# Mixture-of-experts block: experts in units of two or three tiles with the up weights stationary, and one loop body on TensorE

## The reference

```python
x = x + attention(layernorm(x), ctx, ctx)        # 16 heads, projections with bias
xf = layernorm(x).reshape(-1, 256)               # 2048 tokens
probs = softmax(xf @ router_w + router_b)        # 8 experts
top_w, top_idx = top_k(probs, 2)
comb = sum(top_w[..., None] * one_hot(top_idx, 8), axis=1)
out = 0
for e in range(8):
    h = gelu(xf @ expert_up[e].T)                # 256 -> 1024
    out = out + comb[:, e:e+1] * (h @ expert_down[e].T)   # 1024 -> 256
x = x + out.reshape(4, 512, 256)
```

## Time and profile before

| what | us |
|---|---|
| median of three runs (417.35 to 422.19) | 420.72 |
| profiled execution | 422.39 |
| its span | 420.6 |
| PE busy in the span | 385.4 |

### The profile page before, as it was taken

One profiled execution on the slowest core, in us unless ns is written; L12 is line 12 of the kernel. 1 busy time (PEld: TensorE's weight loads), 2 busy tenths in 40 slices (PEclk: granted clock), 3 DMA queues, 4 the chain that ended last, 5 costly groups with the idle time before them and its releaser, 6 DMA issues.

```text
span 420.6 us, 9003 instructions
## 1 busy us (share of the span) xinstructions
PE 385.4 (92%) x2227; PEld 313.0 (74%) x2228; DVE 240.0 (57%) x691; ACT 195.9 (47%) x357; POOL 164.7 (39%) x253
## 2 busy tenths in 40 slices
PE   8989988988988889898999999999999999999960
PEld 6765675665675469896888888888888888888850
DVE  5674776899799767762337636473723643332320
ACT  3545444343434247334447647474734744443420
POOL 2332121211302031146454655655464464546441
PEclk9989999998999999989999999999999999999996
DMA  8912010410221111642326656564632222222121
GB/s 271 348 48 100 0 52 0 153 50 2 71 81 51 51 54 52 199 100 44 52 40 200 169 144 142 137 175 110 196 81 38 38 40 49 37 39 38 38 38 12
DMA packets 26388, 37.22 MB, mean 88 GB/s; under 512 B 4704, under 2 KB 17440, under 8 KB 26368
## 3 DMA queue, kind: packets, MB, share of 16 engines
q1 hardware_dynamic: 19312, 26.98, 18.9%
q0 software_dynamic: 7056, 9.99, 14.8%
HBM read 27.18 MB, written 9.79 MB: 88 GB/s over the span
## 4 chain that ended last, share of the span: by engine, by line
PE 74%; DVE 11%; SPq 4%; ACT 4%; issue 3%; DMA 2%; POOL 1%; POOLq 0%; DVEq 0%; ACTq 0%
PE bankC L1577 14%; PE bankC L1220 10%; PE bankC L1222 10%; PE bankC L1221 10%; PE bankC L1578 7%; PE bankB L1555 6%; PE bankA L1314 2%; PE bankA L1547 2%; PE bankB L1315 1%; PE bankC L1302 1%; DVE nmax L791 1%; DVE put L956 1%; DMA raw<-down 1%; DVE at_l L822 1%; DVE av L817 1%
## 5 line engine op out<-in xcount | busy, mean ns | idle before, releaser
L1577 PE MATMUL bankC<-dn_w,qk_h 128*128 x256 | 94.4, 407 | 1.2 <-DVE qk_l L1155 1.2
L1578 PE MATMUL bankC<-dn_w,qk_l 128*128 x256 | 71.9, 281 | 0.0
L460 POOL DMA_INDIRECT out<-x2T,idx_s x32 | 51.5, 1610 | 18.6 <-issue 18.6
L1577 PEld LDWEIGHTS bankC<-dn_w,qk_h 128*128 128x128 f32 x256 | 48.2, 188 | 11.6 <-issue 1.4
L1220 PE MATMUL bankC<-up_w,xnT_h 128*128 (+1 forms) x128 | 53.1, 415 | 1.0 <-DVE xnT_l L1149 1.0
L1222 PE MATMUL bankC<-up_w,xnT_l 128*128 (+1 forms) x128 | 50.7, 396 | 0.0
L1162 DVE SCALAR_TENSOR_TENSOR x2T<-bankC,gate,x2T 128x256 f32<-128x256 f32 x32 | 15.4, 482 | 61.7 <-ACT x2T L682 52.9
L1221 PE MATMUL bankC<-up_w,xnT_h 128*128 (+1 forms) x128 | 50.6, 395 | 0.0
L1578 PEld LDWEIGHTS bankC<-dn_w,qk_l 128*128 128x128 f32 x256 | 48.2, 188 | 0.0
L677 ACT ACTIVATE raw<-bankC 128x512 f32<-128x512 f32 x64 | 38.4, 599 | 20.3 <-PE bankC L1222 20.3
L450 POOL DMA_INDIRECT xr<-rows,idx_g x35 | 38.9, 1112 | 19.4 <-issue 19.4
(11 more groups left out here) (259 smaller groups left out, 824.1 us busy)
## 6 DMA issues: line engine op xcount, KB each, us to landing
xall<-up SPq DMA_DIRECT2D x24, 256.0 KB
xall<-down SPq DMA_DIRECT2D x24, 256.0 KB
rows<-xr SPq DMA_DIRECT2D x4, 528.0 KB, 3.3
raw<-up SPq DMA_DIRECT2D x4, 512.0 KB, 4.7
raw<-down SPq DMA_DIRECT2D x4, 512.0 KB, 5.3
out<-xall SPq DMA_DIRECT2D x4, 512.0 KB, 2.8
xall<-x SPq DMA_DIRECT2D x1, 1536.0 KB, 9.1
cst<-const SPq DMA_DIRECT2D x1, 640.0 KB, 8.1
```

The source lines that it names most:

```text
L460: g.indirect_dma_start(out, bass.IndirectOffsetOnAxis(idx_s[:, n:n + 1], 0), y[n], None, bounds_check=T + P - 1, compute_op=ALU.add).then_ ...
L1577: mm(bankC[:, 2, :], hT_h[:, o], wd, start=(m == 0), stop=False)
L1578: last = mm(bankC[:, 2, 0:D], hT_l[:, o], wd[:, 0:D], start=False, stop=(m == KF - 1))
```

## The change

Tiles of an expert are grouped: two tiles to a unit, and three in the first unit of an expert with an odd number. Each unit gathers three tiles (a two-tile unit doesn't use the third) and transposes all three. In the up product the weights are stationary and x moves, in 256 or 384 columns, so h comes out with hidden features on its partitions and needs no transposes: per unit 8 x 2 x 3 = 48 matmuls, in four quarters over four banks. ACT takes the gelu twice, rounded to fp32r (high part) and in f32, and DVE subtracts (low part). In the down product the 512-column matmul is split in two of 256, so a tile has 24 matmuls; it accumulates all in one place and ACT's part in the result goes. PE's loop holds one unit: four copies of the up part, one per combination of weight buffer and number of tiles, of which a compare picks one (so their addresses need no registers), two copies of the transposes of x, and a down part per tile with the buffer in a register. The PSUM banks, some buffers, the table and the order of gathers and adds change with it: the third gather of a unit is issued between adds, `add_early(0, 1)` moves behind the first gather, and the first transposes of x move between the two last early down parts.

```diff
-NTAB = NT + 3
+NU = NT // 2
+NTAB = NU + 4
+TRI = 3 * P
...
+        hh, hl = sb("hh", [P, KF * TRI], F32R), sb("hl", [P, KF * TRI], F32R)
...
+        bankC = ps("bankC", [P, 4, 512])
+        bankD = ps("bankD", [P, 2, 512])
+        bankB0, bankB1, bankM = bankC[:, 3, :], bankD[:, 0, :], bankD[:, 1, :]
...
+            def fetch(ring, t):
+                n = 3 * ring + t
+                g.indirect_dma_start(xr[:, n, :], None, rows, bass.IndirectOffsetOnAxis(idx_g[:, n:n + 1], 0),
                                      bounds_check=T + P - 1).then_inc(d_gather[ring], 16)
...
+            def add(u, ring, nth):
+                gather_index(u + 3, 1 - ring, nth)
...
+                pool.wait_ge(d_add, 16 * base + 64)
+                g.tensor_copy(idx_s[:, 3 * ring:3 * ring + 3], slot[:, bass.ds(col, 3)]).then_inc(g_si, 1)
+                pool.wait_ge(g_si, u + 1)
+                pool.wait_ge(v_y, 2 * u + 3)
+                settle(17)
+                give(ring, 0)
+                fetch(1 - ring, 0)
+                pool.wait_ge(v_y, 2 * u + 4)
+                pool.wait_ge(d_add, 16 * base + 80)
+                settle(18)
+                give(ring, 1)
+                fetch(1 - ring, 1)
+                with pool.If(three > 0):
+                    pool.wait_ge(d_add, 16 * base + 96)
+                    settle(19)
+                    give(ring, 2)
+                fetch(1 - ring, 2)
...
             gather(0, 0, 0, col=2)
+            add_early(0, 1)
             pool.wait_ge(v_tab, 1)
+            nu = pool.value_load(nu_i, min_val=NE, max_val=NU)
+            gather(1, 1, 0)
+            add_early(1, 0)
             gather(2, 0, 1)
             add_early(1, 1)
...
+            def gelu(u, n):
+                for q in range(4):
+                    act.wait_ge(p_up, 4 * u + q + 1)
+                    bank = bankC[:, 2 * (q % 2):2 * (q % 2) + 2, 0:n * P]
+                    a.activation(hT_h[:, 2 * q:2 * q + 2, 0:n * P], bank, ACT.Gelu)
+                    a.activation(hbuf[q][:, :, 0:n * P], bank, ACT.Gelu).then_inc(a_gelu, 1)
...
+            def h_low(u, n):
+                for q in range(4):
+                    dve.wait_ge(a_gelu, 4 * u + q + 3)
+                    v.tensor_tensor(hT_l[:, 2 * q:2 * q + 2, 0:n * P], hbuf[q][:, :, 0:n * P],
+                                    hT_h[:, 2 * q:2 * q + 2, 0:n * P].bitcast(F32), ALU.subtract).then_inc(v_fhT, 1)
...
+            def unit(u, ring, nth):
...
+                with dve.If(three > 0):
+                    h_low(u, 3)
+                with dve.Else():
+                    h_low(u, 2)
+                x_low_f(u + 1, 1 - ring, nth)
+                with dve.If(sp_e > 1):
+                    weights_low(sp_e, other, 0)
+                dve.wait_ge(p_dn0, u + 1)
+                dve.wait_ge(d_add, 16 * done + 64)
+                result(ring, 0).then_inc(v_y, 1)
+                with dve.If(sp_e > 1):
+                    weights_low(sp_e, other, 1)
+                dve.wait_ge(p_dn, u + 1)
+                settle(16)
+                with dve.If(three > 0):
+                    result(ring, 2)
+                result(ring, 1).then_inc(v_y, 1)
...
             up_early(1, 3)
             down_early(1, 0)
+            x_turn_f(0, 0)
             down_early(1, 1)
...
+            def up_product(u, par, n):
+                for q in range(4):
+                    pe.wait_ge(a_gelu, 4 * u + q + 1)
+                    for m in (2 * q, 2 * q + 1):
+                        w = slice(m * P, (m + 1) * P)
+                        for k in range(KD):
+                            last = three(bankC[:, 2 * (q % 2) + m % 2, 0:n * P], up_w[:, 0, par, k, w],
+                                         up_w[:, 1, par, k, w], xT_h[:, k, 0:n * P], xT_l[:, k, 0:n * P],
+                                         k == 0, k == KD - 1)
                     last.then_inc(p_up, 1)
+            def down_tile(u, par, t, first):
+                out_ = bankD[:, (t + 1) // 2, t // 2 * D:(t // 2 + 1) * D]
                 for m in range(KF):
+                    if first and m % 2 == 0:
+                        pe.wait_ge(v_fhT, 4 * u + m // 2 + 1)
+                    o = slice(t * P, (t + 1) * P)
+                    w_h, w_l = (dn_w[:, bass.ds(par, 1), m, part, :].rearrange("p a n -> p (a n)") for part in range(2))
+                    mm(out_, hT_h[:, m, o], w_h, start=(m == 0), stop=False)
+                    mm(out_, hT_h[:, m, o], w_l, start=False, stop=False)
+                    last = mm(out_, hT_l[:, m, o], w_h, start=False, stop=(m == KF - 1))
+                return last
...
             pe.wait_ge(v_tab, 1)
+            nu = pe.value_load(nu_i, min_val=NE, max_val=NU)
+            with pe.Fori(0, NU) as u:
+                with pe.If(nu > u):
+                    word = pe.value_load(w_i[:, bass.ds(u, 1)], min_val=0, max_val=4 * NE - 1)
+                    e, three_, par = word // 4, word // 2 % 2, word % 2
+                    pe.wait_ge(v_wlo, 4 * e + 2)
+                    pe.wait_ge(v_fxT, u + 1)
+                    for n in (2, 3):
+                        for p in range(2):
+                            with pe.If(word % 4 == 2 * (n - 2) + p):
+                                up_product(u, p, n)
+                    for ring in range(2):
+                        with pe.If(u % 2 != ring):
+                            x_turn_f(ring, (u + 1) // 2)
+                    pe.wait_ge(v_wlo, 4 * e + 4)
+                    pe.wait_ge(v_y, 2 * u + 2)
+                    with pe.If(three_ > 0):
+                        down_tile(u, par, 2, True)
+                    down_tile(u, par, 0, True).then_inc(p_dn0, 1)
+                    down_tile(u, par, 1, False).then_inc(p_dn, 1)
```

More of the change, by code:

```diff
@@ new lines, in _, with unit @@
+            act.wait_ge(v_tab, 1)
+            nu = act.value_load(nu_i, min_val=NE, max_val=NU)
+            def unit(u):
+                word = act.value_load(split_i[:, bass.ds(u, 1)], min_val=0, max_val=255)
+                sp_e, other, nraw = word // 32, 1 - word // 2 % 2, word // 4 % 8
+                with act.If(word % 2 > 0):
+                    gelu(u, 3)
+                with act.Else():
+                    gelu(u, 2)
+                x_high_f(u + 1)
+                with act.If(sp_e > 1):
+                    weights_high(other, nraw, 0)
+                    weights_high(other, nraw, 1)
@@ L730, in _ @@
+            with act.Fori(0, NU // 2) as i:
+                u = 2 * i
+                with act.If(nu > u):
+                    unit(u)
+                    with act.If(nu > u + 1):
+                        unit(u + 1)
         @block.vector
@@ new lines, in _ @@
+            dve.wait_ge(v_table, 17)
+            for one, part, op in ((te1, on, ALU.add), (tb, onb, ALU.max), (tt, ont, ALU.max), (tpar, onf, ALU.add),
+                                  (tprev, onp, ALU.add), (tthree, onq, ALU.add), (todd, ono, ALU.add)):
+                v.tensor_reduce(one[:, :], part[:, :], AX_X, op).then_inc(v_table, 1)
+            dve.wait_ge(v_table, 24)
+            v.tensor_scalar(tone[:, :], tb[:, :], -1.0, c("tile"), ALU.mult, ALU.add).then_inc(v_table, 1)
+            v.tensor_scalar(tlt[:, :], te1[:, :], float(NE) - 0.5, None, ALU.is_lt).then_inc(v_table, 1)
@@ new lines, in unit @@
+            def unit(u, ring, nth):
+                word = dve.value_load(split_i[:, bass.ds(u, 1)], min_val=0, max_val=255)
+                done = dve.value_load(tbase_i[:, bass.ds(u, 1)], min_val=0, max_val=NT)
+                sp_e, other, three = word // 32, 1 - word // 2 % 2, word % 2
+                with dve.If(three > 0):
[15 more added lines that the diff above has]
+                result(ring, 1).then_inc(v_y, 1)
@@ L1213, in _ @@
+            with dve.Fori(0, NU // 2) as i:
+                u = 2 * i
+                with dve.If(nu > u):
+                    unit(u, 0, i)
+                    with dve.If(nu > u + 1):
+                        unit(u + 1, 1, i + 1)
         @block.tensor
@@ L1538, in _, with x_turn_f @@
             up_early(1, 2)
+            def x_turn_f(ring, nth):
+                pe.wait_ge(d_gather[ring], 48 * (nth + 1))
+                for t in range(3):
+                    for k in range(KD):
+                        last = nc.tensor.transpose(bankA[:, k, t * P:(t + 1) * P],
+                                                   xr[:, 3 * ring + t, k * P:(k + 1) * P], ident)
+                last.then_inc(p_fxT, 1)
             up_early(1, 3)
             down_early(1, 0)
+            x_turn_f(0, 0)
```

454 lines of the change are left out of this document (155 added, 299 removed).

## The result

The changed kernel takes 417.98 us (median of 20 runs, 414.63 to 421.38), the kernel before in the same set 420.4. The ratio is 0.9937, with a 95% interval of 0.9909 to 0.9965: 2.4 us faster, where 10.3 were forecast (410). The profiled execution took 417.45, with a span of 415.7. That is 5.4 us more than the 410.3 that the prediction's sum makes of the profiled span of before.

The account below looks back on a forecast made before the run. PE was taken to bound the expert loop without a gap. Units 188.3 + loop control 12.0 + start 5.6 + end 1.0 = 206.9 instead of 217.2, 10.3 less: 410.4 us; range 398 to 428, forecast's own 402 to 418.

Parts of the forecast that it names:

- start: Ahead of PE's loop: gathered transposes and table waits put the first up product at 194.9 instead of 190.77, +4.1; altogether +5.6.
- loop: PE's expert loop: 188.3 us of units plus 12.0 of loop control, in place of 217.2.
- end: Behind the loop: ACT's low part goes (-0.6), the last add waits for the previous landing, two unused gathers follow: +1.0.
- the wide range: Whole kernel: 398 to 428 us, taking in the first three cases and the foot of the last; forecast's own 402 to 418.
- near 10 us beside PE's 12.9 ... these run two units ahead: nothing: POOL in a two-tile unit: gathers, index copy, adds and pauses near 10 us; waiting for add landings costs nothing.
- PE's products: In the loop: 11.9 us per two-tile unit, 17.5 per three-tile unit, waits included; 188.3 us over 13 units.
- the loop control: PE's path between units, 2.6 us on average, partly hidden by the sequencer's lead: 1.0 idle each, 12 over 12 boundaries.
- fully hidden: Rival at PE's unit boundaries: the sequencer's lead covers the whole path, 12 us go, 398; chance 0.15 (395 to 402).
- no lead: Rival at PE's unit boundaries: waiting for the last h leaves no lead, 1.9 us per unit, 421; chance 0.15 (418 to 424).
- first passes: PE's first passes over new loop code: priced at 1 us, within the start's +5.6.
- Code that doesn't stay: Rival in PE's loop: units wait for refetched code, 443 us with one fetch, 480 with two; chance 0.20, including similar stalls.
- my signs: Profile after: matmul steps, no h transposes, unit periods 12.9 and 18.5, "issue" idle, first loop product near 195, clock 1.00 after 200.

Follow-up runs that it names:

- POOL's edits: Changed kernel with both no gathers past the end and the shorter chain on POOL: 408.58 us with 15 matmuls' shift, 414.54 with 45.
- the shift by 15: Changed kernel with 15 more matmuls at the start of PE's program, so all later code lies further on: 414.18 us, again 414.95.
- the shift by 45: Changed kernel with PE's later code moved by 45 matmuls (15 long ones at the start become 10 long and 50 short): 417.17 us, ratio 0.9928 to the kernel before.
- no gathers past the end: Changed kernel without POOL's index copies, register loads and fetches for units that lie past the end: 412.85 us, ratio 0.9801 to the kernel before.
- the shorter chain on POOL: Changed kernel with the add's index copy and register load moved behind the first add's issue, one register load fewer: 412.89 us, 0.9839 of the kernel before.

## Why the prediction was wrong

The forecast was a clear gain of 10.3 us; 2.4 were measured. Against the profiled span the sum was short by 5.4: start -3.7, loop +1.7, end +7.5 (rounded). That 417.98 still lies inside the wide range, and at the edge of the forecast's own, is luck: none of the rivals has what lengthened the time.

**The step that failed** is POOL's: "near 10 us beside PE's 12.9 ... these run two units ahead: nothing", and with it the end, "+1.0". A two-tile unit takes POOL 12.7 and PE 12.4. The items that I had priced are in the rows near their price or under it: three gathers 3.2 us (4.1 with the pauses ahead of them; I took 4.0), two adds 3.2, an index copy 0.2 (I took 0.9), and 2.2 for the operations on `prime` and the pauses ahead of the adds, for which the sum left 1.9. What I left out is what stands between them on an engine that does one after the other: three register loads (1.89 "issue"), a second index copy (0.19), and 0.95 for the landing of the first add that the gather in front doesn't cover. These 3.0 us, with 0.4 more for pauses and 0.7 less for the first copy, make 12.7 out of 10. The landing that I had put at nothing is the largest of them over the whole loop: 22.5 us of waiting where 5.2 were before, 14.4 of it in the six three-tile units. "Two units ahead" is true of the gathers and says nothing of the adds, which stand behind them on the same engine. And I priced only the two-tile unit: the three adds of the larger unit come in a burst beside the next, shorter unit. So the last adds are late by what POOL still owes, +8.5 us where +1.0 stood. That it is this work is shown by taking some away at the end (tail 14.5), in every unit (15.6), and both (14.7). No row shows that POOL slowed PE itself: with POOL's edits PE's loop takes about as long as without (203.9 and 202.8 beside 203.5, and 200.8 beside 200.9 with the shift by 15). The 14.5 that remain are 1.9 over the 12.6 of before; this is the term that I had priced, the last add behind the landing of the one before it, with 1.9 in place of 1.0.

**PE's products and the loop control** were right in kind. The loop without disturbance, in the shift by 45, takes 198.1 us against 188.3 + 12.0 forecast. The last unit's down products follow each other every 0.119 (45 steps from 389.01 to 394.36), not 0.113 as in the earlier trace rows; over 768 of them that is 4.6 us. Up products follow each other every 0.119 (35 steps from 383.75 to 387.92) and, with 384 columns, every 0.176 (seven steps from 253.68 to 254.91), as forecast. The loop control can be read at the boundaries: from a unit's last down matmul to the next up matmul are 0.12 to 0.81 us, 3.8 us over 12 boundaries beyond the usual step of 0.12, in the changed kernel and in the shift by 45 alike: 0.3 each and not 1.0. Some 1.4 us of the 198.1 stay without a name. So the sequencer's lead hides more than I gave it, and the rival "fully hidden" was nearer than the forecast; the rival "no lead" is out.

**The start.** From the last write of the slots to the first up product it is 14.2 us (176.89 to 191.13), against 10.7 before (180.10 to 190.77): +3.6, close to the +4.1 of the forecast. The slots themselves were written 3.2 us earlier in this execution than in the one that the prediction used, where the clock from 178 to 182 was 0.64; here it is 1.00 in that stretch. (That stretch isn't thin, as the prediction has it: PE is busy for all its 4.00 us; thin is the one ahead of it, 174 to 178, with 2.71.) In another execution (no gathers past the end) they were written at 180.8 and the first up product came at 195.2. So this gain of 3.2 isn't shown to be the change's. The first unit took 18.2 us (to the first up product of the second at 209.32), for which I had set 11.9, and 1 for first passes; in the shift by 45 it took 12.8. So 5.4 us, as much as 203.5 is over 198.1, go to the fetch and to the slow clock on both sides of it; I had set 1.5.

**Code that doesn't stay** is out: the 48 later branches take at most 0.233 us and no packet follows. The Trainium skill (Runtime: NRT & Kernel Launch, section Instruction fetch mechanics) says that a taken branch to a page that isn't held waits for its fetch: the first pass agrees, with 3.10 us. Of the two figures that the Trainium skill gives there for PE's room, 2,048 instructions and two lines of 16 KiB, the later passes agree with the first and not with the second, by the prediction's estimate of 650 instructions, three packets, for this body.

Of my signs two speak against the forecast: the clock of 0.68 behind 202 us, and the first loop product at 191.13 and not near 195. The others hold: the up steps, no transposes of h, a two-tile unit every 12.4 to 13.0 and a three-tile unit every 17.9 to 18.6, idle PE put down to "issue", no packets through the loop. None of them asked after the engine that failed. The row to ask for was POOL's waiting for results: 48.8 us before, 3.0 per two tiles, of which PE's shorter unit (12.4 for 13.4) took 1.0 and POOL's added work the rest.

## What to carry to other kernels

When the engine that bounds a loop gets faster, add up each other engine's whole period per pass, with register loads, index copies, pauses and waits for landings, in the order in which one engine must do them; an engine that is busy 43% of the time can still be the slowest. Read how long it waits for the bounding engine now: that is all the room there is, and where results come in larger groups, what is still owed behind the last group is paid at the end. A jump into code for the first time is worth a look in any loop with alternative bodies, and an edit that shifts code can gain or lose some microseconds that have nothing to do with its purpose, so compare by stage and try the shift alone.

## What the runs showed of the hardware

The first taken branch over code that hadn't been fetched held PE's sequencer for 2.94 to 3.18 us in the four traces without a shift (changed kernel twice, and each of POOL's two edits alone), for 1.65 to 2.07 in the five with 15 matmuls more ahead of it, and for 0.35 in the two with 45 more. The later branches took at most 0.233. In the changed kernel the loop was 5.4 us longer for its first passes than in the shift by 45: PE stood still for 2.9, and the rest went in the stretches behind the two pauses of 2.88 us, one ahead of the loop and one at the branch, where the granted clock was 0.62 and 0.68 (0.57 and 0.72 when it was run again); in the shift by 45 it was 1.00 throughout the loop. What makes it fall isn't settled: in the 4 us from the first up product on, which the same pause of 2.88 to 2.90 us precedes, it was 0.58 to 0.64 in five traces (the changed kernel twice, no gathers past the end, POOL's two edits with either shift) and 1.00 in four (the shorter chain on POOL, the shift by 15 twice, the shift by 45).

An indirect DMA occupied POOL for 1.0 to 1.1 us per gather of 128 rows and 1.6 per add in the last units, with 0.3 of pause in between; where an add waited for the landing of the one before it and little stood between them, as without gathers past the end, the adds of the last units were issued 4.6 to 5.5 us apart.
